# A two-layer network on one core: the queries of two heads in one product, three steps for a query, five read-outs on ScalarE, and the expert tiles in longer runs

## What is computed

```python
x = L0_attn_x                              # 8 rows of 512 tokens, 128 channels, f32
xn = _layernorm(x)
x = x + L0_attn(xn) + L0_ffn(xn)           # layer 0
xn = _layernorm(x)
x = x + L1_attn(xn) + L1_ffn(xn)           # layer 1
# L1_attn: 16 heads, each with its own queries, keys and values common to all heads
q = (x @ Wq + bq).reshape(B, S, H, DK)     # H = 16, DK = 64
k = x @ Wk + bk
v = x @ Wv + bv
scores = jnp.einsum('bshd,btd->bhst', q, k) / sqrt(DK)
out = jnp.einsum('bhst,btd->bshd', softmax(scores), v)
return out.reshape(B, S, H * DV) @ Wo + bo
# L1_ffn: a gate picks 2 of 8 experts for each token (hidden width 512)
h = jax.nn.gelu(jnp.einsum('bsf,efh->bseh', x, W1) + b1)
expert_out = jnp.einsum('bseh,ehf->bsef', h, W2) + b2[None, None]
return jnp.einsum('bsef,bse->bsf', expert_out, selected)
```

## Time and profile before

| | before |
|---|---|
| median of 3 runs | 1476.2 us (1471.74 to 1479.75) |
| profiled execution, its time | 1480.48 us |
| its span, first to last instruction | 1478.6 us |
| granted TensorE clock, mean | 0.963 of full |
| TensorE busy | 91% of the span |
| VectorE busy | 76% |
| ScalarE busy | 47% |

### The profile page before, as it was taken

The page is one execution under the profiler, slowest core; times in us unless marked ns, Lnnn a source line. Parts: engine busy times, 40 slices in busy tenths (PEclk is TensorE's granted clock), DMA queues, the critical chain, the costliest instruction groups (busy, mean ns, idle before and its releaser), DMA issues.

```text
span 1478.6 us, 18582 instructions
## 1 busy us (share of the span) xinstructions
PE 1346.8 (91%) x5393; PEld 900.9 (61%) x5393; DVE 1117.6 (76%) x2736; ACT 694.4 (47%) x1185; POOL 230.4 (16%) x283
## 2 busy tenths in 40 slices
PE   4579999999999999999999999999999699989995
PEld 2346565666666656665666666666666466767653
DVE  8786888688868886888688867886787476756582
ACT  2126454534454445444544454445444457657542
POOL 4112213100120012001200120001001042443400
PEclk9569999999999999999999999999999899999998
DMA  3402433200020003000200020000000455454152
GB/s 104 96 13 92 144 118 110 78 16 23 20 83 16 23 20 82 18 23 19 80 16 26 19 80 16 27 16 27 16 19 22 152 178 169 158 186 137 60 139 62
DMA packets 68881, 100.05 MB, mean 68 GB/s; under 512 B 25584, under 2 KB 45616, under 8 KB 64816
## 3 DMA queue, kind: packets, MB, share of 16 engines
q1 hardware_dynamic: 56400, 70.73, 15.7%
q0 software_dynamic: 10192, 27.44, 6.1%
q10 hardware_dynamic: 2192, 0.71, 0.2%
HBM read 60.14 MB, written 38.44 MB: 67 GB/s over the span
## 4 chain that ended last, share of the span: by engine, by line
PE 58%; DVE 21%; issue 12%; POOL 5%; DMA 2%; ACT 1%; SPq 1%; POOLq 0%; DVEq 0%; ACTq 0%
PE bank L1313 21%; PE bank L1293 6%; PE bank L1247 6%; PE bank L1294 6%; POOL y_rows L616 5%; DVE mneg L891 5%; PE bank L1329 4%; PE bank L1157 2%; PE bank L1159 2%; PE bank L1158 2%; DVE q_lm L885 2%; PE bank L1208 1%; PE bank L1190 1%; DVE on L1086 1%; PE bank L1198 1%
## 5 line engine op out<-in xcount | busy, mean ns | idle before, releaser
L720 ACT ACTIVATE wide<-bank 128x512 f32<-128x512 f32 x512 | 304.4, 598 | 544.9 <-PE bank L1294 503.4
L1313 PE MATMUL bank<-wide,v_w 128*128 128x512 f32 x1024 | 526.1, 596 | 0.0
L891 DVE TENSOR_REDUCE mneg<-bank 128x1 f32<-128x512 f32 x512 | 348.2, 688 | 121.7 <-PE bank L1247 97.6
L1293 PE MATMUL bank<-q_hh,k_hl 128*128 128x512 f32 x512 | 366.5, 716 | 2.1 <-ACT wide L720 1.1
L1247 PE MATMUL bank<-k_hl,q_hh 128*128 128x512 f32 x512 | 206.9, 406 | 17.1 <-DVE mneg L891 13.5
L1313 PEld LDWEIGHTS bank<-wide,v_w 128*128 128x128 f32 x1024 | 189.6, 191 | 47.2 <-issue 1.4
L597 POOL DMA_INDIRECT x_rows<-xr,slot_u x64 | 67.8, 1059 | 891.7 <-DVE slot_u L972 740.2
L1294 PE MATMUL bank<-q_lm,k_h 65*128 65x512 f32 x512 | 202.2, 395 | 0.0
L1293 PEld LDWEIGHTS bank<-q_hh,k_hl 128*128 128x128 f32 x512 | 97.4, 190 | 99.6 <-issue 93.2
L1294 PEld LDWEIGHTS bank<-q_lm,k_h 65*128 65x128 f32 x512 | 97.8, 191 | 92.8 <-issue 90.3
L885 DVE SCALAR_TENSOR_TENSOR q_lm<-bank,bq,q_hh 64x512 fp32r<-64x512 f32 x128 | 94.7, 740 | 61.9 <-ACT q_hh L669 58.1
(11 more groups left out here) (230 smaller groups left out, 1858.4 us busy)
## 6 DMA issues: line engine op xcount, KB each, us to landing
w_t<-w_rows SPq DMA_DIRECT2D x23, 1024.0 KB
x_rows<-part_h POOLq DMA_DIRECT2D x65, 258.0 KB, 4.9
inv<-inverse_scratch SPq DMA_DIRECT2D x128, 128.0 KB
w_rows<-w_t SPq DMA_DIRECT2D x8, 1024.0 KB, 4.7
x_m<-x_rows SPq DMA_DIRECT2D x23, 258.0 KB
yab<-in_L_ffn_W SPq DMA_DIRECT2D x16, 256.0 KB, 5.0
yab<-y_rows SPq DMA_DIRECT2D x8, 512.0 KB, 4.3
xin<-in_L_attn_x SPq DMA_DIRECT2D x8, 256.0 KB, 3.2
```

The costliest lines, as they stand in the source:

```text
L720: act.activation(wide[:, st.g % WIDE, :], ps, ACT.Exp, scale=SCALE1).then_inc(wide_full, 1)
L891: dve.tensor_reduce(mneg[:, (gh // 2) % 2, col:col + 1], ps[:], X, ALU.max, negate=True)\
L1293: pe.matmul(ps, k_hl[:, n, t], q_hh[:, gh % HEADS, :], start=True, stop=False)
L1313: last = pe.matmul(ps_out[b][:], v_w[:, st.r % 2, c, :], wide[:, st.g % WIDE, :], start=(c == 0), stop=(c == TT - 1))
```

## The change

**Queries.** `query` makes the queries of two heads (an even head and the next) in one product, at c = 1 of every even head: 64 partitions hold the one, 64 the other. A bank of its own holds the result until both are read out; the ring of the others has three banks. ScalarE rounds head gh of the pair one and two steps after, in two activations of 64x512 into the two halves of `q_hh`; VectorE makes the rest two and three steps after the product. `HEADS` goes from 4 to 6.

```diff
+            i = banks - 1 if name[0] == kind else n % (banks - 1)
+            n += name[0] != kind
...
-    HEADS = 4
+    HEADS = 6
+    QUERY_AT = 1
...
-    INSERT = {7: 5, 15: 6, 19: 6, 23: 6}
+    INSERT = {15: 8, 19: 8, 23: 7}
...
-    LAST_AFTER = ATT + 24
+    LAST_AFTER = ATT + 6
+    DIRECT = 12
+    INVERSE_AT = {DIRECT: 58, DIRECT + 1: 62, DIRECT + 2: 65, DIRECT + 3: 67}
+    LAST_NORM_AT = {8: 60, 9: 61, 10: 63, 11: 64, 12: 64, 13: 65, 14: 66, 15: 67}
+    LAST_WO_AT = [None, ATT + 1, ATT + 4]
...
-    BEGIN_AT = {46: "xt", 48: "k", 49: "v", 50: "gl", 58: "rk"}
+    BEGIN_AT = {46: "xt", 48: "k", 50: "vg", 58: "rk"}
...
-    COMBINE_AT = [38 + 3 * n for n in range(NB)]
+    LANDED_AT = 34
+    COMBINE_AT = [39 + 3 * n for n in range(NB)]
...
-        if c == TT - 1 and 0 <= gh + LEAD + 1 < H * NB:
-            events.append(("q", gh + LEAD + 1))
+        if c == QUERY_AT and h % 2 == 0 and 0 <= gh + LEAD + 1 < H * NB:
+            events.append(("q", (gh + LEAD + 1) // 2))
...
-                act.activation(q_hh[:, gh % HEADS, :], ps[:], ACT.Identity, bias=bq[:, gh % H:gh % H + 1])\
...
-            def query(gh):
-                n, h = divmod(gh, H)
-                into(("q", gh), lambda ps: three(ps[:], twice(wq_h[:, h]), twice(wq_l[:, h]),
-                                                 x_h[:, n % 2, :], x_l[:, n % 2, :]))
+            def query(pair):
+                n, i = divmod(pair, H // 2)
+                if i == 0:
+                    read_out(pe, ("xt", n))
+                into(("q", pair), lambda ps: three(ps[:], wq_h[:, i, :], wq_l[:, i, :], x_h[:, n % 2, :], x_l[:, n % 2, :]))
...
-                    if st.kind == "o" and st.k == 3:
+                    if st.kind == "o" and st.k == 9:
                         for t in range(XT):
                             load_tile_rows(t)
...
-                            if st.k == COMBINE_AT[n] - (3 if n < 2 else 2):
+                            if st.k == LANDED_AT:
                                 load_landed(n)
...
+                if r == NB - 1:
+                    for o, at_ in INVERSE_AT.items():
+                        if k == at_:
+                            gh = H * r + o
+                            emptied(dve, group_of[gh])
+                            dve.reciprocal(inv_d[0:DK, o - DIRECT, :], raw[DK:, gh % RAW, :]).then_inc(inverted_d, 1)
```

More of the change, by code:

```diff
@@ L186, in head_events, with split_heads, wo_at, norm_at @@
         return events
+    def split_heads(st, after):
+        if st.kind not in ("pre", "o"):
+            return None
+        at_ = TT * (H * st.r) + st.k - QUERY_AT - after
+        pair, b = divmod(at_, 2 * TT)
+        gh = 2 * pair + LEAD + 1 + b
+        return gh if b < 2 and 0 <= gh < H * NB else None
+    def wo_at(r, part):
+        if part == 0 or r < NB - 1:
+            return WO_AT[part] if part < 2 else None
+        return LAST_WO_AT[part]
+    def norm_at(r):
+        at_ = dict(enumerate(NORM_AT))
+        if r == NB - 1:
+            at_ = {**at_, **LAST_NORM_AT}
+        return at_
     def project_events(st):
-        return [("wo", r, half) for r, k in row_steps(st) for half in range(2) if k == WO_AT[half]]
+        return [("wo", r, part) for r, k in row_steps(st) for part in range(3) if k == wo_at(r, part)]
     def l0_events(st):
@@ L668, in round_q, with copy_m @@
                     act.wait_ge(first_full, g_of[r, TT * h + TT - 1] + 1)
[L669 to L670 removed]
+                rows = slice(DK * (gh % 2), DK * (gh % 2) + DK)
+                for half in range(2):
+                    last = act.activation(q_hh[DK * half:DK * half + DK, gh % HEADS, :], ps[rows, :], ACT.Identity,
+                                          bias=bq[rows, gh % H:gh % H + 1])
+                last.then_inc(qh_done, 1)
+            def copy_m(pair):
+                ps, free = filled(act, ("mt", pair))
+                act.wait_ge(m_loaded[pair % 2], pair // 2 * 16)
+                act.activation(mrow[:, pair % 2, :], ps[0:2 * TT, 0:P], ACT.Identity).then_inc(free, 1)
             def begin(use, n):
+                if use == "xt":
+                    ps, _ = filled(act, ("xt", n))
+                    act.activation(x_h[:, n % 2, :], ps[:], ACT.Identity).then_inc(xh_done, 1)
                 if use == "k":
                     ps, _ = filled(act, ("k", n))
[L675 removed]
+                    act.activation(k_hl[:, n % 2, :], ps[:], ACT.Identity, bias=bk[:, 0:1])
+                    act.activation(k_h1[0:DK, n % 2, :], ps[0:DK, :], ACT.Identity, bias=bk[0:DK, 0:1]).then_inc(k_rounded, 1)
             def turned_weight(n):
@@ L1062, in row_end @@
             def row_end(r, k):
-                for half in range(2):
-                    if k == WO_AT[half] + 1:
+                for half in range(3):
+                    if wo_at(r, half) is not None and k == wo_at(r, half) + 1:
                         ps, free = full(("wo", r, half))
-                        if half or r == NB - 1:
+                        if half == 2:
+                            read_out(dve, ("wo", r, 1))
+                        elif half or r == NB - 1:
                             kept()
@@ L1108, in _ @@
             for st in steps:
+                if split_heads(st, 2) is not None:
+                    lo_q(split_heads(st, 2))
                 if st.kind in ("pre", "o"):
```

198 lines of the change are left out of this document (101 added, 97 removed).

## The result

The changed kernel takes 1566.1 us (median of 4 runs, 1565.91 to 1566.87), the kernel before 1474.19 us beside it (1471.74 to 1479.75): ratio 1.062, 95% interval 1.0585 to 1.0652. I had forecast 1437, and had given one mechanism on the slower side 1 chance in 20. The profiled run took 1566.87 us.

What follows compares the result with a forecast made beforehand. TensorE was taken as the bound, with VectorE binding in some stretches of a row. Terms -36 - 4 - 3.5 - 14 + 17.5 + 11.5 - 11 = -39.5 us from 1476.2 gave 1437 us, range 1408 to 1462.

Steps and rivals of the forecast that it cites:

- the one on the ring: Rows 0 to 6: three shared banks in place of four for all but queries make TensorE wait 0.5 us a row.
- the three banks stop TensorE: Rival, rows 0 to 6: late VectorE turns TensorE's savings into waits for mneg; 1504 us, chance 0.05.
- Queries: Rows 0 to 6: 8 queries fewer a row at 0.71 us each take 5.7 us off TensorE.
- 5.1 us a row: Rows 0 to 6: net gain per row, 7.0 - 1.4 - 0.5, seven rows -36 us.
- my first rival: Rows 0 to 6: VectorE stands closer behind TensorE, each row saves 2.5 us, 1455 us; chance 0.20.
- Read-outs on ScalarE: Rows 0 to 6: five read-outs leave VectorE for ScalarE, about 6.5 us a row off VectorE.
- Cost nothing: Rows 0 to 6: ScalarE's added roundings (11 us a row) and read-outs cost nothing, covered by its idle 40%.
- Start: Steps ahead of row 0, at half clock: fewer matmuls, queries and read-outs save 4 us (2 to 5).
- First tile: Row 7: TensorE's 12.67 us wait for the first tile's rows and slow products behind it go, -14 us.
- Longer runs: Row 7's expert tiles: 11 waits for y_rows in place of 7, one run fewer; +17.5 us (12 to 24).
- The eight loads: Row 7: eight 512 KB loads at k = 34 delay the maxima row needed at k = 40; +11.5 us (0 to 16).
- Tail: From k = 40 of row 7 to the end: 57.6 us against 68.7, -11 us (5 to 18).

Runs made afterwards that it cites:

- four banks: As a run: the changed kernel, paired queries, all uses sharing four banks in turn, both heads read out in the query's own step; 1467.4 us.
- single queries: The changed kernel with queries of one head each and all uses in four banks, all else as changed; 1471.8 us.
- three banks alone: The kernel before with one edit: one-head queries get a bank of their own, all else shares three banks; 1522.5 us.

## Why the prediction was wrong

**The step that failed** is the one on the ring: "It was seldom so late; I take 0.5 us a row for it." Measured, it is 13.2 us in a full row (160.4 against 147.2 with nothing but the banks changed) and 12.1 on average, 85 us in rows 0 to 6 and 97 over the kernel. I asked how often VectorE was late with four banks, where the waits of the earlier trace rows's kernel are few, and took the few waits for a slack. They were few since the fourth bank covered strings of up to 3 us; with one bank less the strings at k = 32, 46 and 54 end in waits. What had to be read was VectorE's timeline between maxima, not TensorE's waits. And the wait was priced bare; in the trace 3.04 us of it cost 4.9, since the matmuls behind it ran at a granted clock of 0.69. The rival "the three banks stop TensorE" was the right mechanism, but priced at 1504 us and at a chance of 0.05; the argument against it (over the row TensorE idles 4.6 us in all) is the same mistake.

**Queries.** The 0.71 us each was right, by the steps that lose or gain a query. That 5.1 us a row arrive was wrong even with four banks: rows 0 to 6 fall by 13.5 us, 1.9 a row, and by 12.5 with single queries. The pairing alone gives 0 in a full row and 4 to 5 us in all, most of it in the start. That VectorE stands closer behind than I count was my first rival (2.5 us a row); it is closer still. The merged product of values and gate logits was right: TensorE is busy 1.1 us less in a row with single queries (143.03 against 144.12), where I had 1.3.

**Read-outs on ScalarE**: counted inside the row's 5.1, measured as 21 us with four banks. They take 39.5 us off VectorE over the kernel, 4.9 a row, where I had 6.5. The two roundings of 64x512 at 681 ns each are at the full price, as taken: here a half of the partitions cost what all had cost, 687 ns for 128x512, and ScalarE's row is 84 us busy against my 86. "Cost nothing" holds in part: with four banks TensorE waits 10 us for ScalarE's hqt behind the roundings, in 16 waits.

**Start**: -1.0 in place of -4 with three banks, and -4.4 with four (106.2 against 110.6 us to row 0); with single queries it is -0.3 (110.3), so what it gains is the pairing's.

**First tile**: the 12.67 us went, but 9.9 us came back as another wait. In the changed kernel TensorE stops at k = 8 for the maxima row of heads 2 and 3, queued behind four tiles' weights, which SyncE issues from 1227.48 on (timeline of TensorE, and of SyncE's queue around it):

```profile
1244.54 0.77 PE L1349 MATMUL bank<-q_hh,k_hl 128*128 128x512 f32 x1 [9.89 <-DMA q_lm<-mrow]
```

```profile
1235.81 0.34 SPq L508 DMA_DIRECT2D w_t<-w_rows  x1
...
1237.41 0.34 SPq L475 DMA_DIRECT2D sums_scratch<-raw  x1
1242.18 0.34 SPq L479 DMA_DIRECT2D sums<-sums_scratch  x1
1242.57 0.72 SPq L458 DMA_DIRECT2D q_lm<-mrow  x1
```

Here the sums' return load goes 4.77 us after their store, where such waits were 1.44 on average before. The weights were there before too, and held up the same row: it was issued at 1164.11, after the wait of the earlier trace rows. But then TensorE had five tiles to do between k = 7 and k = 8 (the step k = 7 took 36.9 us with them), so the row was there in time. With the tiles behind k = 15 nothing covers it any more. "What is late next is the loop of the tiles" was wrong: -3 us remained of -14.

**Longer runs**: 11 waits for y_rows as worked out, 41.6 us as worked out (41); by the steps k = 15 to 27 the cost is some 13 us, at the lower part of 12 to 24. ScalarE has two ACT_TABLE_LOADs fewer, 1.28 us each, where I had 1.5 us for the run that went.

**The eight loads**: the wait at k = 40 came, for the reason given, with 6.10 us where I had 10; with the clock behind it (0.50 from 1501.0 to 1506.5) +7.7 in place of +11.5. SyncE's queue:

```profile
1486.67 7.01 SPq L528 DMA_DIRECT2D yab<-y_rows  x8
1493.72 1.05 SPq L475 DMA_DIRECT2D sums_scratch<-raw  x1
1500.11 0.34 SPq L479 DMA_DIRECT2D sums<-sums_scratch  x1
1500.49 0.70 SPq L458 DMA_DIRECT2D q_lm<-mrow  x1
```

The maxima row was there when TensorE went on at 1502.45, 15.8 us after the first load's issue, where I had some 20. So the 2.1 us per load were somewhat too high. Seven of these us SyncE spent on issuing the loads; the sums' return load goes 6.4 us after their store, against 3.54 behind one load. No run tells how many of the eight were still in flight then.

**Tail**: -6.3 us in place of -11, so 62.4 us from k = 40 on where I had 57.6. The four reciprocals took 3.35 us each, by VectorE's groups, where I took 3.3:

```profile
L1133 DVE RECIPROCAL inv_d<-raw 64x512 f32<-64x512 f32 x4 | 13.4, 3348 | 0.1
```

The slope of the small ones was a good guide: 6.9 ns an element there, 6.5 here (3348 ns for 512). VectorE's work came out smaller than my 50.3 us, but the one us of waits between it was wrong. The stretch from k = 40 to the end of its last product for the projection (columns as in the earlier trace rows):

```profile
1502.50:1557.85 55.35, 47.65 (x167) 30.04 (x167) 48.85 (x95) 20.76 (x37) 0.00 (x0) 0.93 0.18 54
```

VectorE is busy 48.85 of 55.35 us and idle 6.5, of which 4.3 stand at k = 40 to 42, for the maxima products of a TensorE that has just waited for the row, and 1.5 for the projection's first half. Behind its last product 7.05 us pass where I had 6.5, with the last quarter of the projection (3.68 us) at a granted clock of 0.54. The 5.93 us of the earlier trace rows were at 0.63, a little above the half that I had written.

**The account.** By the spans the change costs 86.3 us, the forecast was -39.5: a gap of 126. Rows 0 to 6 hold 117 of it: 85 are the ring, 10 the read-outs spread over three steps, 22 the gains that don't arrive with four banks either (-13.5 in place of -36). Row 7 and the tail hold 6 (+6.5 for +0.5), the start 3.

**Where the pairing's time goes with four banks** can be read by steps, row 4 with single and with paired queries. At k = 19 and 27 the maxima product waits 0.65 us for ScalarE's hqt behind the roundings, at k = 45 and 53 the maxima's transpose waits 0.92 and 0.42 for VectorE, at k = 58 the ranks wait 1.17 for ScalarE's x0t. These five steps are 4.9 us longer than the pairing's count makes them, out of 5.7 us that it takes off a row, and the steps behind the wait at k = 33 are 1.6 longer, at a granted clock of 0.75 and 0.78 where the single queries have 1.00 behind the same wait of 1.6 us; k = 39 and 59 get some 2 back.

**What stays open**: why a wait of 1.6 to 2.1 us is followed by the slow clock in some rows and not in others, and how much of the 33 us by which pairs make three banks worse (85 against 52) is VectorE's lost time to catch up. No run took either apart.

## What to carry to other kernels

A buffer's depth must be judged by the longest string of other work on the engine that empties it, not by how often it is waited for now: with few waits shown, one buffer less can cost nothing or all. Price a wait on TensorE with the slow clock that may follow it: here 3.04 us of wait cost 4.9. And where a large wait or a stretch of work is moved, look in the trace for what was due during it: it may stand there as the next wait.

## What the runs showed of the hardware

- Behind a wait of 3.04 us the 32 matmuls of a projection took 5.44 us in place of 3.73, in each of five rows, at a granted clock of 0.69. Behind a wait of 1.93 us (three banks alone) they were slow in three rows (a step of 8.94 us) and at full clock in three others (7.30); behind 1.86 to 1.88 us (the run with layer 0's pieces moved) slow in three rows and at full clock in two; behind 0.75 us (k = 21 of the changed kernel) the step was 6.24 us in all six rows, at full clock.
- One execution had a granted clock of 0.75 from 200 to 1100 us with TensorE busy 98% of the time, and took 1677 us where the same kernel took 1564 the other time. Its cause was not found.
- An activation of 64x512 took 681 ns (256 of them), one of 128x512 took 687 (128 of them).
- A reciprocal of 64x512 took 3.35 us on VectorE (four of them).
- SyncE took 7.0 us to issue eight loads of 512 KB. The sums' return load went 6.4 us after a small store issued behind them, 3.5 us behind one such load.
